# A six-block decoder on one core: the routing shares are turned one expert step later, and the second self attention takes its softmax sums from a block of ones on TensorE

## What is computed

```
# third block: every token goes through all 8 experts, weighted by its two routing shares
gate_scores, expert_idx = jax.lax.top_k(tokens @ gate_w.T, 2)
combine = zeros((T, E)).at[arange(T)[:, None], expert_idx].add(softmax(gate_scores))
for each expert: acc += c[:, None] * (gelu(tokens @ W1.T + B1) @ W2.T + B2)
# fourth block: 16 heads of 8 features
scores = einsum('bhqd,bhkd->bhqk', q, k) / sqrt(8)
probs = softmax(scores, axis=-1)
out = einsum('bhqk,bhkd->bhqd', probs, v) -> (B, S, 128) @ Wo + bo
```

## Time and profile before

| what | value |
|---|---|
| median of 3 runs | 2250.47 us (2249.54 to 2250.77) |
| the profiled execution, its own time | 2251.52 us |
| its span, first to last instruction | 2249.7 us |
| TensorE matmuls busy | 1986.1 us (88%) |
| VectorE, ScalarE, GpSimd busy | 1406.2 us (63%), 1287.7 us (57%), 453.3 us (20%) |
| mean granted TensorE clock | 0.943 of full speed |

### The profile page before, as it was taken

One profiled execution on the slowest core, in us unless ns is written; L12 is line 12 of the kernel. 1 busy time (PEld: TensorE's weight loads), 2 busy tenths in 40 slices (PEclk: granted clock), 3 DMA queues, 4 the chain that ended last, 5 costly groups with the idle time before them and its releaser, 6 DMA issues.

```text
span 2249.7 us, 47403 instructions
## 1 busy us (share of the span) xinstructions
PE 1986.1 (88%) x16072; PEld 1496.5 (67%) x16072; DVE 1406.2 (63%) x3578; ACT 1287.7 (57%) x4657; POOL 453.3 (20%) x784
## 2 busy tenths in 40 slices
PE   3639999999999999998699999799996775989987
PEld 1228888888888888886476767566654554556555
DVE  4776777777777777775466565577764773342442
ACT  2216776667777776665244444599996892333332
POOL 1110111111111111111212120244442331110110
PEclk8769999999999999998799999799997995999999
DMA  7000000000000000001000000100000000000000
GB/s 219 11 0 2 2 1 2 2 2 2 1 2 2 2 2 2 2 2 51 16 1 1 1 1 1 34 2 2 2 2 24 13 5 1 1 10 0 9 9 9
DMA packets 27232, 25.40 MB, mean 11 GB/s; under 512 B 3068, under 2 KB 23556, under 8 KB 27016
## 3 DMA queue, kind: packets, MB, share of 16 engines
q1 hardware_dynamic: 27016, 22.62, 3.6%
HBM read 20.52 MB, written 2.10 MB: 10 GB/s over the span
## 4 chain that ended last, share of the span: by engine, by line
issue 62%; PE 14%; POOL 8%; ACT 7%; POOLq 6%; DVE 1%; DMA 1%; DVEq 0%; ACTq 0%; SPq 0%
PE bank L1962 5%; ACT work L1487 5%; POOL work L949 2%; PE bank L1972 2%; PE bank L1422 2%; ACT work L1495 1%; POOLq L952 1%; POOL H L953 1%; POOL work L937 1%; POOL work L1042 1%; PE bank L1989 1%; PE bank L1431 1%; POOLq L1833 1%; POOLq L1831 1%; POOL work L1823 1%
## 5 line engine op out<-in xcount | busy, mean ns | idle before, releaser
L817 ACT ACTIVATE work<-bank,work 128x128 f32<-128x128 f32 x1024 | 364.6, 405 | 223.9 <-DVE work L870 223.9
L697 PE MATMUL bank<-work,wbig 128*128 128x128 f32 x2048 | 262.0, 276 | 0.6 <-ACT work L858 0.5
L817 ACT ACTIVATION_READ_ACCUMULATOR work<-bank,work 128x1 f32 x1024 | 250.5, 245 | 0.0
L697 PEld LDWEIGHTS bank<-work,wbig 128*128 128x128 f32 x2048 | 245.7, 193 | 1.2 <-ACT work L858 0.8
L877 DVE TENSOR_TENSOR work<-work 128x512 f32<-128x512 f32 x256 | 177.3, 693 | 19.5 <-issue 0.5
L870 DVE TENSOR_REDUCE work<-bank 128x4 f32<-128x512 f32 x256 | 159.0, 684 | 33.7 <-PE bank L736 33.7
L1487 ACT ACTIVATE work<-bank,work 128x128 f32<-128x128 f32 x512 | 176.1, 347 | 4.3 <-DVE work L1523 4.3
L832 ACT ACTIVATE work<-bank 128x512 f32<-128x512 f32 x256 | 170.5, 667 | 13.3 <-PE bank L710 13.3
L710 PE MATMUL bank<-ident,work 128*128 128x128 f32 x1024 | 156.3, 275 | 3.1 <-DVE work L877 3.1
L1962 PE MATMUL bank<-work,wbig 128*112 128x320 f32 x512 | 151.0, 439 | 8.5 <-DVE work L2060 5.3
L1176 ACT ACTIVATE work<-bank,col_b 128x512 f32<-128x512 f32 x128 | 87.2, 687 | 104.0 <-PE bank L1104 104.0
(11 more groups left out here) (283 smaller groups left out, 4098.3 us busy)
## 6 DMA issues: line engine op xcount, KB each, us to landing
wbig<-in_moe_w SPq DMA_DIRECT2D x2, 1792.0 KB, 9.8
work<-in_mask_l SPq DMA_DIRECT2D x8, 256.0 KB, 2.9
out<-X SPq DMA_DIRECT2D x4, 512.0 KB, 3.2
H<-in_moe_w SPq DMA_DIRECT2D x1, 1792.0 KB, 9.4
wff<-in_moe_w SPq DMA_DIRECT2D x1, 1024.0 KB
wbig<-in_sa_wq SPq DMA_DIRECT2D x1, 512.0 KB, 3.7
wbig<-in_sa_wk SPq DMA_DIRECT2D x1, 512.0 KB, 4.6
wbig<-in_sa_wv SPq DMA_DIRECT2D x1, 512.0 KB, 5.6
```

Of the source, the lines that this page charges most:

```text
L697: last = nc.tensor.matmul(o[:, j * T:(j + 1) * T], w[:, t * 128:(t + 1) * 128], src, start=True, stop=True)
L817: last = nc.scalar.activation(at_probs[:, g, h, :], bank[g][:, h * T:(h + 1) * T], ACT.Exp, bias=at_nmax[:, g, h:h + 1], accum_out=at_den[ ...
```

## The change

In the first mixture `shares_in` moves on TensorE from the end of step 6 to step 7, between `up(n, 7)` and `down`, and on ScalarE from behind the gelu of step 6 to behind that of step 7. In self attention the sums of the exponentials are no longer taken by ScalarE. TensorE multiplies the turned exponentials by a block that has ones in the 8 columns of head `s` (`l1_ones`), sixteen more products of the form of L1442, so that each sum stands in bank 7 already turned and spread over its head's rows. The copy in `heads` becomes a reciprocal of 128x128 in PSUM. Out go the small reciprocal, its transposition, its copy and the product with `l1_expand`. Eight small memsets make the block of ones at the start of the stage.

```diff
@@ -1127,6 +1125,8 @@
                         ff_up(n + 2, 1)
                     if first and e == 2:
                         ff_up(n + 2, 2)
+                    if second and e == 7:
+                        shares_in(n + 1)
                     if k >= 1:
                         down(k - 1)
                     if first and e == 2:
...
@@ -1137,8 +1137,6 @@
                         tokens_in(n + 1)
                     if second and e == 4:
                         logits(n + 1)
-                    if second and e == 6:
-                        shares_in(n + 1)
                     if second and e == 7:
                         bias(n + 1)
             down(EXPERTS - 1)
...
@@ -1391,20 +1387,14 @@
                 need(pe, l1.v_sb, min(t, B - 1) + 1)
                 need(pe, l1.res_sum, t - 1)
                 need(pe, l1.xT_sb, min(t + 3, B))
-                if t + 3 < B:
-                    last = nc.tensor.transpose(bank[7][:, 0:T], X[:, t + 3, :], ident[:])
-                if 1 <= t <= B:
-                    pe.wait_ge(l1.recips, t)
-                    last = nc.tensor.transpose(bank[7][0:HEADS, T:2 * T], l1_recip[(t - 1) % 2], ident[:])
-                if t + 3 < B or t >= 1:
-                    last.then_inc(l1.turned, 1)
+                nc.tensor.transpose(bank[7][:, 0:T], X[:, t + 3, :], ident[:]).then_inc(l1.turned, 1)
 
             def project(b):
                 xT = l1_xT[b % 3]
...
@@ -1435,14 +1425,15 @@
                 turned1(pe, b, TURNED_ON_DVE)
                 turned1(pe, b, 3)
                 pe.wait_ge(l1.xT_sb, min(b + 4, B - 1) + 1)
-                pe.wait_ge(l1.recipT_sb, b + 1)
                 pe.wait_ge(l1.v_sb, b + 1)
-                for s in range(QUAD):
-                    for j in range(QUAD):
-                        nc.tensor.matmul(bank[7][32 * j:32 * j + 32, 0:T], l1_v[b % 3][:, s, 32 * j:32 * j + 32],
-                                         l1_probsT[b % 2][:, j, s, :], start=(s == 0), stop=(s == QUAD - 1),
-                                         skip_group_check=True)
-                nc.tensor.matmul(bank[7][:, T:2 * T], l1_expand, l1_recipT, start=True, stop=True).then_inc(l1.pv, 1)
+                for k, weights in enumerate((None, l1_v[b % 3])):
+                    for s in range(QUAD):
+                        for j in range(QUAD):
+                            w = weights[:, s, 32 * j:32 * j + 32] if k else l1_ones[:, s, :]
+                            last = nc.tensor.matmul(bank[7][32 * j:32 * j + 32, (1 - k) * T:(2 - k) * T], w,
+                                                    l1_probsT[b % 2][:, j, s, :], start=(s == 0), stop=(s == QUAD - 1),
+                                                    skip_group_check=True)
+                last.then_inc(l1.pv, 1)
 
             def output(t):
                 if 1 <= t <= B:
...
@@ -1485,8 +1477,7 @@
                 need(act, l1.probsT, QUAD * (b - 2) + g + 1)
                 for h in range(QUAD):
                     last = nc.scalar.activation(l1_probs[b % 2][:, g, h, :], bank[g][:, h * T:(h + 1) * T], ACT.Exp,
-                                                bias=l1_nmax[b % 2][:, g, h:h + 1],
-                                                accum_out=l1_den[b % 2][:, QUAD * g + h:QUAD * g + h + 1])
+                                                bias=l1_nmax[b % 2][:, g, h:h + 1])
                 last.then_inc(l1.probs, 1)
 
             def turned(b, g):
...
@@ -1522,11 +1510,6 @@
                 dve.wait_ge(l1.scores, 2 * b + g // 2 + 1)
                 nc.vector.tensor_reduce(l1_nmax[b % 2][:, g, :], bank[g][:, :].rearrange("p (h t) -> p h t", h=QUAD),
                                         AX.X, ALU.max, negate=True).then_inc(l1.maxes, 1)
-
-            def recip(b):
-                dve.wait_ge(l1.probs, QUAD * (b + 1))
-                need(dve, l1.turned, b + 3)
-                nc.vector.reciprocal(l1_recip[b % 2], l1_den[b % 2]).then_inc(l1.recips, 1)
 
             def turned(b):
                 dve.wait_ge(l1.probsT, QUAD * b + TURNED_ON_DVE + 1)
...
@@ -1546,9 +1529,9 @@
             def heads(b):
                 dve.wait_ge(l1.pv, b + 1)
                 need(dve, l1.out_ready, b)
-                nc.vector.tensor_copy(l1_headsT, bank[7][:, 0:T])
-                dve.drain()
-                nc.vector.tensor_tensor(l1_headsT, bank[7][:, T:2 * T], l1_headsT, ALU.mult).then_inc(l1.heads_sb, 1)
+                nc.vector.reciprocal(l1_recip, bank[7][:, T:2 * T])
+                dve.drain()
+                nc.vector.tensor_tensor(l1_headsT, bank[7][:, 0:T], l1_recip, ALU.mult).then_inc(l1.heads_sb, 1)
 
             def values(b):
                 dve.wait_ge(l1.v, b + 1)
...
@@ -1589,12 +1572,16 @@
-            nc.vector.tensor_copy(l1_expand, bank[5][0:HEADS, 2 * T:3 * T]).then_inc(l1.tables_sb, 1)
+            for k in range(QUAD):
+                nc.vector.memset(l1_ones[:, k, :], 0.0)
+            dve.drain()
+            for k in range(QUAD):
+                last = nc.vector.memset(l1_ones[:, k, DH1 * k:DH1 * (k + 1)], 1.0)
+            last.then_inc(l1.tables_sb, 1)
             dve.drain()
             for t in range(-2, B + 1):
                 now = 0 <= t < B
                 if t >= 1:
-                    recip(t - 1)
                     turned(t - 1)
                 if now:
                     greatest(t, 2)
```

More of the change, by code:

```diff
@@ L242, in build @@
             xT_sb = sem("l1_xT_sb")
-            recipT_sb = sem("l1_recipT_sb")
             qk = sem("l1_qk")
@@ L249, in build @@
             probs = sem("l1_probs")
-            recips = sem("l1_recips")
             probsT = sem("l1_probsT")
@@ L1349, in build @@
         l1_wturned = r.take(2, D)
-        l1_expand = r.take(D, parts=HEADS)
+        l1_ones = r.take(QUAD, 4 * DH1)
         l1_xT = [r.take(T) for _ in range(3)]
@@ L1358, in build @@
         l1_nmax = [r.take(QUAD, QUAD) for _ in range(2)]
-        l1_den = [r.take(HEADS) for _ in range(2)]
-        l1_recip = [r.take(HEADS) for _ in range(2)]
-        l1_recipT = r.take(T, parts=HEADS)
+        l1_recip = r.take(T)
         l1_headsT = r.take(D)
@@ L1393, in tables @@
                 for k in range(2):
-                    nc.tensor.transpose(bank[5][:, k * T:(k + 1) * T], l1_turn[:, k, :], ident[:])
-                nc.tensor.transpose(bank[5][0:HEADS, 2 * T:3 * T], headmask[:, :], ident[:]).then_inc(l1.tables_ready, 1)
+                    last = nc.tensor.transpose(bank[5][:, k * T:(k + 1) * T], l1_turn[:, k, :], ident[:])
+                last.then_inc(l1.tables_ready, 1)
             def tokens(t):
@@ L1466, in attn1_pe @@
                     turn(t - 1, 3)
-                tokens(t)
+                if t + 3 < B:
+                    tokens(t)
                 if 0 <= t + 2 < B:
@@ L1499, in tokens @@
                 act.wait_ge(l1.turned, t + 4)
[L1500 to L1504, removed]
+                nc.scalar.activation(l1_xT[(t + 3) % 3], bank[7][:, 0:T], ACT.Copy).then_inc(l1.xT_sb, 1)
             for t in range(-3, B + 1):
```

## The result

The changed kernel takes 2230.14 us (median of 4 runs, 2228.97 to 2231.37) against 2250.62 us before (2249.54 to 2251.18): ratio 0.991, 95% interval 0.9892 to 0.9927, 20.5 us faster.

The account below looks back on a forecast made before the run. TensorE's waits for routing shares bound the first mixture, ScalarE the self attention turn. 11.1 us (10.3 + 0.8) plus 3.9 us (28 x 0.14) gave 15.0 us off, 2235.5 us; own range 2233 to 2238.5, overall 2231 to 2243.

Parts of the forecast that it names:

- What bounds: First mixture: TensorE, with waits for routing shares; self attention: ScalarE sets the 7.86 us turn, TensorE's own work 7.40.
- The move: First mixture: `up(n, 7)` runs under the wait for routing shares, gaining 1.72 us in six loops, 10.3 us; 0.5 us remain.
- Loop 0's clock: First mixture, loop 0: with less idleness TensorE's clock may hold, worth 1.63 us more; half, 0.8 us, was booked.
- TensorE's exchange: Self attention: transposition and L1445 out (0.11 and 0.42 us), sixteen products in (0.85); TensorE's turn 7.40 becomes 7.72 us.
- ScalarE: Self attention: sixteen exponentials without sums, 0.25 us each for 0.34, give back 1.5 us; about 5.7 us a turn.
- VectorE: Self attention: the 128x128 reciprocal takes 0.95 us, and `output` does not wait for VectorE, by 0.2 us.
- Weight loads: Self attention: loads of the new products overlap with products as in L1442, at 0.026 us an instruction.
- my rival: Self attention: loads and sums do not overlap, turn 0.67 us longer, 20 us lost, 2259.4 us; chance 0.05.
- these I book at zero, plus or minus 1.5: Self attention: relief of some 0.5 us in each of two last turns, against longer last chain and memsets, booked at zero.
- The rival that had it: More than forecast: clock holds in loop 0 and self attention's first turns, 2 to 3 us more, 2233 us; chance 0.07.

Follow-up runs that it names:

- the run without sums: Kernel before, exponentials taking no row sums (constant 128 instead, old path kept; softmax sums left out): 2232.09 us, ratio 0.9915.
- the run with the sums kept: Kernel before with the block of ones but not the move, ScalarE still taking row sums that nothing reads: 2253.32 us, ratio 1.0008.
- the move alone: Kernel before with the routing shares moved behind `up(n, 7)`, self attention unchanged: 2238.37 us, ratio 0.9941.

## Why the prediction was right in most of its steps and low in its sum

- *What bounds.* Right in the first mixture. In self attention the bound is as I said, but TensorE's own turn is 7.34 us and not 7.40: the wait cost 0.53 us and not the 0.46 of idle time shown. The transpositions in front of it last 0.60 us, while the next group starts 0.53 behind them in the run without sums; the difference is not in the idle time.
- *The move.* 1.72 us a loop forecast, 1.71 measured. The wait left was to be 0.5 and is 0.38. `bias` and `ff_up` wait no more than 0.2 us.
- *Loop 0's clock.* I took half of 1.63 us. This term was mis-sized: every profile with the long waits has one slow loop, none with the short ones has any, so it was a whole, 1.6 us.
- *TensorE's exchange.* Out 0.53 and in 0.85 forecast, 0.32 net; in 0.87 and 0.35 net measured.
- *ScalarE.* The pitch without sums is the 0.25 us taken. ScalarE is busy 152.04 / 192 x 7.69 = 6.1 us of a turn, where I had 5.7. The relief is needed, as the run with the sums kept shows. The Trainium skill's estimate of 294 ns ("ScalarE: Activation LUTs", What ACT_TABLE_LOAD costs) is above this case's 250 from one start to the next.
- *VectorE.* 0.95 us forecast, 0.96 measured; slack 0.2 forecast, 0.13 found.
- *Weight loads.* By the Trainium skill ("TensorE: Matmul & The Clock Gate", The mechanism) loads for tiles of the same rows should not hide under products in flight; the same section excepts loads into a background buffer, which my rival left out. The trace disagrees with the rule as I used it, at 0.027 us for a load and a product.
- *The step that failed.* "these I book at zero, plus or minus 1.5": the two ends of self attention gave 6.3 us between the profiles. What I had weighed there was nearly right. Between the move alone and the changed kernel, whose starts are alike, the first two turns give 0.9 us and the last two 0.5; in the very end the steps up to the last `weigh` are 1.0 shorter and those from it to `output` 1.1 longer at like clock. That is 1.3 us, within the 1.5. What failed is that this sum held TensorE's clock at nothing: in the profile before, the fall in the second turn costs 3.1 us and the lower level at the very end 1.9 (partly an estimate, as said above), together 5.0.
- *The rival that had it.* "The clock holds in loop 0 and stays up in the first turns of self attention: 2 to 3 us more", with a chance of 0.07, named two of the three places. It was priced too low: loop 0 gave 0.8 more than booked, the first turns 3.1 and the end, which it did not name, 1.9.

Put together, the work moved and removed gives 10.3 + 4.6 + 1.3 = 16.2 us, and the clock 1.6 + 5.0 = 6.6 in these two profiles; blocks that no edit touches take 0.5 back. The median is 20.5 and not 22.4 us lower: the profiled execution before lies 1.0 us above its median, the one of the changed kernel 1.2 below. What share of the runs of each kernel has a long turn is open. The mean clock is a hint only: 0.944 or 0.945 in the four runs of the changed kernel's result, 0.942 in the one whose profile shows the late rise.

## What to carry to other kernels

When two engines are level, moving work from one to the other pays only through the wait that it removes. Here relieving ScalarE is worth 0.53 us a turn, and the sums on TensorE take 0.35 of it back; without the relief, the same sums gain nothing. Put an independent group under each wait for a long chain on another engine, and look for the next wait in the same way; price it by what the group in front of it costs with and without the wait, and not by the idle time shown. Do not book the clock at the ends of a stage at zero. They are where waits and the clock meet, and two profiles of one kernel differ by 3.6 us there for no edit at all. Compare the granted clock of two profiles before you put a difference at their ends down to an edit.

## What I had not expected of the hardware

Idle time of TensorE in the trace is less than the wait costs: 0.46 us shown against 0.53, and 0.38 against 0.55. A stage that starts at the lower clock can rise to the higher one 10 us sooner or later in two profiles of one program (granted clock 1.00 and 0.50 in the window from 1425 to 1430), and it can rise and fall again for 6.8 us while TensorE still has work (0.50 from 1443 to 1449). Waits of 2.09 us in each loop brought one fall of the clock in each of six profiles, worth 1.6 to 1.7 us, behind the wait of loop 0 in three and of loop 2 in three; waits of 0.38 us brought none in six.
